# Row scatters that wait for the end of the one ahead: 128 indirect DMAs on GpSimd in a state-space mixer with routed experts

## The reference, cut to what matters

```python
x = L0_attn_x                                # 32 x 256 tokens of 128 elements, f32
xn = _layernorm(x, axis=-1)
x = x + mixer(xn, ...) + experts(xn, ...)

# mixer: in-projection to 2 x 256, causal convolution of 4 taps, silu,
#        dt = softplus(...), alpha = sigmoid(0.1 dt), h = scan(alpha, gated) over each 256 tokens,
#        y = (h * C_gate + D * x_conv) * silu(z), out-projection to 128
# experts:
logits = xt @ w_gate                         # 8192 x 8
top_logits, sel = jax.lax.top_k(logits, 2)
probs = jax.nn.softmax(top_logits, axis=-1)
h = silu(xt @ w1[e]) * (xt @ w3[e]); y = h @ w2[e]     # 8 experts, hidden 256
out = sum over the 2 chosen experts of probs * y
```

## Time and profile before

| | before |
|---|---|
| median of three runs | 474.22 us |
| the profiled execution | 472.82 us |
| its span | 471.0 us |
| PE busy | 428.5 us (91%) |
| DVE busy | 394.9 us (84%) |
| ACT busy | 289.3 us (61%) |
| POOL busy | 311.1 us (66%) |
| the 128 scatters into the regions, L593 | 36.6 to 210.5 us, 132.3 us busy |
| the expert stage begins on PE | 216.6 us |

### The profile page before, as it was taken

One profiled execution on the slowest core, in us unless ns is written; L12 is line 12 of the kernel. 1 busy time (PEld: TensorE's weight loads), 2 busy tenths in 40 slices (PEclk: granted clock), 3 DMA queues, 4 the chain that ended last, 5 costly groups with the idle time before them and its releaser, 6 DMA issues.

```text
span 471.0 us, 8361 instructions
## 1 busy us (share of the span) xinstructions
PE 428.5 (91%) x2440; PEld 306.9 (65%) x2440; DVE 394.9 (84%) x836; ACT 289.3 (61%) x406; POOL 311.1 (66%) x344
## 2 busy tenths in 40 slices
PE   0889969999999999998999999999999999989771
PEld 0877524555545555554888889889888998644461
DVE  5999985999999999997998997767767775699981
ACT  2793476788898888899364444344444553878710
POOL 3657777777777777660377777777777777776300
PEclk9999999999999999999999999999999999999997
DMA  8951126122121313143667766566556662019996
GB/s 244 290 174 43 52 101 188 52 66 81 52 92 51 97 52 97 35 119 109 171 204 218 231 203 191 177 186 189 168 159 188 179 181 89 21 52 226 210 214 147
DMA packets 48078, 65.93 MB, mean 140 GB/s; under 512 B 8424, under 2 KB 30223, under 8 KB 48048
## 3 DMA queue, kind: packets, MB, share of 16 engines
q1 hardware_dynamic: 36240, 39.56, 30.1%
q0 software_dynamic: 10656, 24.47, 18.6%
q10 hardware_dynamic: 1152, 1.57, 1.1%
HBM read 42.09 MB, written 33.83 MB: 161 GB/s over the span
## 4 chain that ended last, share of the span: by engine, by line
PE 48%; DVE 33%; issue 11%; ACT 5%; DMA 1%; DVEq 0%; SPq 0%; ACTq 0%
PE PD L893 13%; DVE hbuf L1398 6%; PE PB L725 4%; DVE hbuf L1409 4%; PE PD L836 3%; PE PA L859 3%; PE PB L855 3%; PE PA L855 3%; PE PB L859 3%; PE PB L856 3%; PE PA L856 3%; DVE gbuf L1380 3%; DVE y L1418 2%; DVE gbuf L1283 2%; DVE xacc L1496 2%
## 5 line engine op out<-in xcount | busy, mean ns | idle before, releaser
L608 POOL DMA_INDIRECT moe_out<-xnT,dst_u x142 | 147.2, 1036 | 63.4 <-issue 33.7
L593 POOL DMA_INDIRECT moe_in<-xn,slot_u x128 | 132.3, 1034 | 44.6 <-issue 39.1
L1196 ACT ACTIVATE xn<-PA 128x1024 f32<-128x1024 f32 (+1 forms) x36 | 36.5, 1015 | 64.3 <-PE PA L859 54.9
L893 PE MATMUL PD<-xnT,xn 128*128 128x128 f32 x536 | 65.7, 275 | 0.0
L1623 DVE TENSOR_TENSOR xn<-xn,PB 128x1024 f32<-128x1024 f32 (+1 forms) x36 | 43.4, 1205 | 25.5 <-PE PB L859 20.5
L893 PEld LDWEIGHTS PD<-xnT,xn 128*128 128x128 f32 x536 | 62.8, 192 | 0.5 <-issue 0.5
L740 PE MATMUL PC<-xc,Wc 128*128 128x512 f32 x128 | 57.8, 594 | 2.9 <-ACT xc L1093 2.9
L753 PE MATMUL PA<-xnT,Wtap 128*128 (+4 forms) x128 | 58.2, 598 | 0.0
L753 PEld LDWEIGHTS PA<-xnT,Wtap 128*128 128x128 f32 x128 | 24.9, 194 | 31.6 <-issue 31.6
L740 PEld LDWEIGHTS PC<-xc,Wc 128*128 128x128 f32 x128 | 23.2, 190 | 26.8 <-issue 23.4
L1486 DVE SCALAR_TENSOR_TENSOR acc<-PA,cw,acc 128x510 f32<-128x510 f32 (+2 forms) x48 | 35.5, 740 | 1.8 <-ACT acc L1082 1.4
(11 more groups left out here) (244 smaller groups left out, 922.9 us busy)
## 6 DMA issues: line engine op xcount, KB each, us to landing
xnT<-moe_w SPq DMA_DIRECT2D x36, 256.0 KB
xn<-moe_in SPq DMA_DIRECT2D x31, 266.0 KB
out_dram<-moe_out POOLq DMA_DIRECT2D x12, 512.0 KB, 15.3
xnT<-moe_w SPq DMA_DIRECT2D x36, 128.0 KB, 2.1
out_dram<-xacc SPq DMA_DIRECT2D x7, 512.0 KB, 3.5
moe_out<-xnT,dst_u POOLq DMA_INDIRECT x142
moe_in<-zrow SPq DMA_DIRECT2D x8, 266.0 KB, 3.5
moe_w<-in_L_ffn_w_dram SPq DMA_DIRECT2D x2, 1024.0 KB
```

Of the source, the lines that this page charges most:

```text
L593: gp.indirect_dma_start(xs_dram, bass.IndirectOffsetOnAxis(ap=slot_u[:, k, j:j + 1], axis=0), xn_row[:, j, :], None).then_inc(s_scat, 16)
L608: gp.indirect_dma_start(yt_dram, bass.IndirectOffsetOnAxis(ap=dst_u[:, t, j:j + 1], axis=0), yo[t % OUTS][:, j, :], None, bounds_check=lim ...
L893: last = pe.matmul(PD[:, 512 + j * D:512 + (j + 1) * D], hid[b][:, k * SLOTS + j * P:k * SLOTS + (j + 1) * P], (w2x[t - FULL] if mixed and ...
L1196: act.activation(halves(sil, t), halves(PA[:, :], t), ACT.Silu).then_inc(s_sil, 1)
```

## The change

Each scatter into the regions gets a second semaphore, `s_desc`, which GpSimd itself counts up by one when it has completed the instruction (`engine_sem`); `s_scat` is counted by the DMA as before. Ahead of every scatter but the first, behind the wait of `follow`, stands a wait until `s_desc` has reached the number of the scatters issued so far (`BEHIND` is 1). The second loop of indirect DMAs (L608) stays as it is.

```diff
+BEHIND = 1
...
+        s_desc = sem("s_desc")
...
                 for j in range(q0 * QT, (q0 + qn) * QT):
                     for k in range(TOP_K):
                         follow(j * TOP_K + k)
+                        if j * TOP_K + k >= BEHIND:
+                            gp.wait_ge(s_desc, j * TOP_K + k + 1 - BEHIND)
                         gp.indirect_dma_start(xs_dram, bass.IndirectOffsetOnAxis(ap=slot_u[:, k, j:j + 1], axis=0),
-                                              xn_row[:, j, :], None).then_inc(s_scat, 16)
+                                              xn_row[:, j, :], None, engine_sem=s_desc).then_inc(s_scat, 16)
```

## The result

| | before | after |
|---|---|---|
| median of the runs on one chip (4 each) | 474.45 us | 527.15 us (526.64 to 527.35) |
| ratio | | 1.112, 95% interval 1.110 to 1.115 |
| the profiled execution, its span | 472.82, 471.0 us | 527.35, 525.5 us |
| end of the last scatter | 210.45 us | 265.83 us |
| first expert transpose on PE | 216.62 us | 270.31 us |

On one chip the kernel before and three kernels of the experiments (ten late waits, ten early waits, one small write) took 543 to 564 us, and the ratios given from there compare the three with that kernel before.

A forecast was written before the change was run, and what follows sets the result against it. It took the chain over DVE, PE and ACT to bound the kernel, the scatters having slack. 472.8 + 52.9 (later stream end less slack) + 1.9 (restart) = 527.6, median 1.4 above: 529.0 us; own range 516 to 540, 8 in 10 512 to 550.

The forecast's parts named there:

- step 2: Scatters 21 to 127: the new wait, second of two, becomes a sequencer instruction; gap 0.77 us, 0.47 more than now.
- step 3: Scatters 21 to 38: 31.1 us of periods, 1.05 for one long scatter, 4.2 waiting for DVE; scatter 39 at 101.2.
- step 5: Last 33 scatters, DVE idle from about 218 on: last begins 55.4 us later, at 264.1 to 264.3, ends at 265.2.
- Step 1: Scatters 1 to 20, with the new wait alone: gap 0.31 us against 0.30 now, 0.2 us in all.
- late count: Rival for the scatters' gap: completion counted some 0.2 us behind the span's end; gap 1.0, 546 us, chance 9%.
- short preparation: Rival: L593, with no bound to check, is prepared faster than L608; gap 0.50 to 0.65, 516 to 524 us, chance 12%.
- the sequencer's lead of nine scatters: POOL's sequencer works some nine scatters ahead, hiding its work; the new wait, standing second, ends that.
- The windows: Spans of each DVE step delaying scatters' row-number fetches: 0 to 1.22, 4.19 to 6.52, 7.92 to 9.29, 9.33 to 10.56 us.
- Step 4: Scatters 39 to 94: locked to DVE, seven a step of 13.44 us (12.1 and 1.33 waiting), eight steps to 208.7.
- Step 6: Start of experts: the last scatter may end 1.9 us later free (slack); TensorE's slow clock after idling adds 1.9 (restart).
- The rival of the other side: Mixer steps: spacing the scatters' fetches frees DVE, at most 4.6 us, so 469.6 us; chance 3%.

The follow-up runs named there:

- ten late waits: Against the kernel before, new wait only ahead of the last ten scatters: ratio 1.001 on the slow chip; on another chip 480.56 against 474.51 us, ratio 1.0108.
- ten early waits: Against the kernel before, new wait only ahead of scatters 21 to 30: ratio 0.995 on the slow chip; on another chip 477.89 against 474.51 us, ratio 1.0060.
- one small write: Against the kernel before, no counter or wait; GpSimd writes one element per partition ahead of each scatter from 21 on: ratio 1.001 (0.995 to 1.008).
- the wait first: Against the changed kernel, the new wait stands ahead of the wait of `follow`: 473.35 us against 473.71 of the kernel before, ratio 0.9988.
- the first two experiments: Against the changed kernel: new wait put ahead of that of `follow`, 473.35 us; or kept behind it but for the last scatter but one, 473.49 us.
- two runs with writes: Against the kernel before, no completion count; GpSimd writes 256 or 384 elements per partition ahead of each scatter from 21 on: 504.90 and 522.64 us.
- the writes of 384: Against the kernel before, no completion count; GpSimd writes 384 elements per partition ahead of each scatter from 21 on: 522.64 us, ratio 1.1010.
- the writes of 256: Against the kernel before, no completion count; GpSimd writes 256 elements per partition ahead of each scatter from 21 on: 504.90 us, ratio 1.0638.
- two behind: Against the changed kernel, `BEHIND` is 2, so each scatter waits for the completion of the last but one: 473.49 us, ratio 0.9997.
- the counter alone: Against the changed kernel, the new wait is removed; `s_desc` is counted and nothing waits for it: 473.99 us, ratio 1.0012.
- two small writes: Against the kernel before, no completion count; GpSimd makes two writes of one element per partition ahead of each scatter from 21 on: 474.17 us, ratio 0.9992.

## Why the prediction was right, step by step

The mechanism held, but for one detail (step 2), and the time by it (529.0 for 527.15, and 527.6 for the profiled execution's 527.35). Some sizes were off, and that the sum came within 0.3 us of this execution is in part luck: step 3 was 2.8 too large and step 5 was 3.5 too small.

Step 1, scatters 1 to 20: 0.31 forecast, 0.30 in the trace. The completion count isn't late, and the rival "late count" is out: the sequencer's wait runs 0.02 behind the end of the scatter.

Step 2, 107 waits in the sequencer and a gap of 0.77: 107 and 0.78. The gap taken from the second loop's L608 held although L597 checks no bound, so "short preparation" is out. The experiments on the order and on the distance of the wait show the cause: between the sequencer's wait and the start of the scatter behind it lie 0.73 us, and they are hidden when the wait can be passed before the scatter ahead ends. The detail that did not hold is that the sequencer's lead of nine scatters is what hides them: with the wait first the lead is gone too and nothing is lost, so a lead of one is enough. The Trainium skill, page "Perfetto Trace Analysis", section "Identifying Dependency Chains", says that an instruction which waits on several engines may have EventSemaphore instructions put ahead of it for the further conditions; the trace agrees, with 107 of them. Their number isn't their price: the 107 of the changed kernel cost 52.7 us, the 107 of each of the first two experiments nothing. What the sequencer does in the 0.73 us no row shows.

Step 3, scatter 39: forecast 101.2, in the trace 98.43. This term was too large by 2.8. All waiting for DVE, that of scatter 31 (1.61 long) with it, was 2.3 us, where I had 4.2 and another 1.05 for one long scatter. The windows themselves held: stepping through them again from scatter 21 at 64.87 with a gap of 0.78 and DVE's first step at 78.01, its place in this trace, puts scatter 39 at 98.4 (98.9 with the step at 76.79, as before the change); this is an estimate, but from the same windows. The check that I had on it was weaker than I wrote: for the kernel before my stepping ended 1.2 us early, and I put that down to the hole of scatter 113, but this hole is 2.84 beyond a normal gap, so without it the stepping was already some 1.6 late. The long scatter doesn't belong to scatter 31: with the early waits two others were long, at 78.77 (1.82) and at 83.90 (1.93).

Step 4, seven a step: right, from 98.43 to 206.00 there are 56 scatters in eight steps. The two runs with writes support the windows behind it.

Step 5, the last 33: forecast 55.4 from the first to the last start, measured 58.87. The missing 3.5 are mostly the hole of scatter 113, 2.75 beyond a normal gap; I had named one hole of some 3 us in the stream and left it out of the sum. The rest is 0.2 from the gap of 0.78 and some 0.5 in which scatter 96 still waited for DVE. Together with step 3 the stream's end came at 265.83 instead of 265.2, +55.4 for +54.8.

Step 6, slack and restart: 1.69 in this trace (1.81 in that of the late waits) for 1.9, and 0.77 for the restart for 1.9. The restart was mis-sized, though not by its kind: from the first transpose to `down` the traces show 10.04 before, 10.36 with 2.6 us of idle time, 10.81 here, and 11.88, 12.10 and 12.12 with the writes of 384, the late waits and those of 256. So 1.9 is within what a restart costs, and here the clock came back sooner: the granted clock is 1.00 from 276 on, 5.7 behind the first transpose, while with the writes of 256 it is still 0.50 from 250 to 252 and 1.00 only from 254 on, 8.6 behind. Why the clock comes back at different moments stays open.

Net: +0.6 in the stream's end, +0.2 in the slack, -1.1 in the restart: 527.3 for 527.6. The median lay 1.4 above the profiled execution before and 0.2 below it after, which makes 1.6 of the 1.9 us between 529.0 and 527.15. The rival of the other side, a DVE freed by spaced fetches, is out too: DVE's step stayed 13.45 us.

## What to carry to other kernels

Where a DMA on GpSimd gets a second wait, the first one written rides on it and the next is an instruction of the sequencer; met only when the DMA ahead ends, it cost 0.48 us each time here. So put first the one that is satisfied last, above all a wait for the engine's own instruction just ahead, or wait for the one before it. Read a gap's price against the rhythm of the engine it meets: a stream that by DVE's windows has some 0.04 us to spare in a step of 13.44 lost two of its ten scatters in each step to 0.19 us a gap. A delay that leaves PE idle has a restart in its price too, here 0.3 to 2.1 us.

## What the runs showed of the hardware that was not expected

GpSimd's small writes fit into the gap between two scatters at no cost: the gap is 0.30 without them, 0.31 with one write of 0.12 and 0.31 with two of 0.15 together. A longer write pushes the next scatter out: 0.33 gives a gap of 0.49 and 0.43 one of 0.60, each the write and 0.17.

Scatter 113 has a hole in every trace, whatever stands around it: 3.14 before, 3.53 after, 3.14 to 3.30 with the wait first, two behind and the counter alone, 2.75 to 3.17 in the others. It stays with the instruction and not with the time (190.80 before, 240.52 after). No row shows what it waits for; its cause is open.

The clock's dip in the opening of the mixer stage was longer after the change (0.90, 0.50 and 0.74 in three stretches of 4 us from 64 on, where before it was 1.00, 0.60 and 0.98), and the mixer's step 11 came 1.27 us later. The stream of the scatters hid this. The new wait isn't needed for it: with the counter alone the same stretches show 0.88, 0.50 and 0.77 and the mixer 1.02 later, with two small writes 0.98, 0.50 and 0.67 and 1.50 later, and both kernels take the time of before. In these two traces the end of the stream is later by the same 1.02 and 1.50: the locked stream goes along with DVE. Why the dip is longer in some traces stays open.
